# A Mamba block and a mixture of experts on one core: the steps of a chunk's projections, turns, norms and scatters laid out anew

## The chip, the cores and the metric

One core of one Trainium2 chip. The metric is the device time of one execution in microseconds, the median of the runs shown. The core has TensorE (matmuls and transposes, results to PSUM), VectorE, ScalarE (called ACT here), GpSimd, and a queue that issues DMAs (SyncE). Each engine works off its own instructions strictly in the order in which they were given, and waits on semaphores that the others raise.

## The reference

Input x is 8 sequences of 1024 tokens with 256 features, f32. Two stages follow each other:

```
n   = layernorm(x)                         # without weights
h   = layernorm(n, ln_g, ln_b)
x_in, z = split(h @ W_in)                  # 256 -> 2 x 512
u   = silu(causal_conv(x_in, 4 taps) + conv_b)
dt, B, C = split(u @ W_xproj)              # 64 + 16 + 16
delta = softplus(dt @ W_dt + b_dt)
s_t = exp(delta_t * A) * s_(t-1) + delta_t * B_t * u_t     # 512 channels x 16 states
y_t = sum over states of s_t * C_t, + u * D_param
x1  = x + n + (y * silu(z)) @ W_out
r   = layernorm(x1)
out = x1 + layernorm(r + top-2-of-8 experts(r), gamma, beta)
```

Routing takes the two largest of eight logits of `r` and weighs two experts (256 to 512, relu, back to 256) with a softmax of the two.

## The kernel before

**Chunks, groups and steps.** `mamba_block` cuts the tokens into 16 chunks of 512 (`NC`). An even chunk begins a sequence, an odd one goes on with it, so its scans start from states that the even one saved (`carry`). A chunk has four groups of 128 channels (`G`), a group has 16 states (`N`). One state of one group over 512 tokens is one scan instruction on VectorE, so a chunk has 64 steps (`SG`), numbered here 0 to 63. Step 19, say, is state 3 of group 1. GpSimd has half steps (two states at once, `HB` = 8 for a group, 32 for a chunk). Each engine runs its own written-out loop over the steps (`for at in range(STEPS)`); the step at which an instruction is given fixes only its place in that engine's order. Time comes from the waits.

**What a step needs.** For scan n, ACT makes the decay `exp(delta * A)` (`exp_a`, L1053). GpSimd makes the product with B for two states (`times_b`, L764), but not for states 4, 5, 10 and 11: their products come from TensorE ("drives", L1343, of `duT` and the diagonals `dg`). VectorE scans (L612). The states are weighed with C: ten of 16 by VectorE in five instructions (`weigh`, L624), six by GpSimd in three (L781; called W0, W1 and W2 here, given at the half steps of `WEIGH_P`; W2 needs scan 15 of its group and is given in the next group's half steps). TensorE turns each weighed pair into `ps_y` by eight transposes ("turn 0" to "turn 4" of VectorE's pairs, `TURN_D`, and of GpSimd's, `TURN_P`). `begin_y` (`SKIP_Y`) starts `ps_y` with the skip term, called y0 here. When all eight turns of a group are in, VectorE's `gate` (L634, state 3 of the next group) multiplies `ps_y` with silu(z). The product delta * u of the next group (`times_u`, L751, called U) is on GpSimd, given at half step `DU_AT`; it is transposed by TensorE ("turnu").

**The two slots of ps_p.** Everything else on TensorE goes through two PSUM banks in turn (`proj`, by place in `table`; `emptied` tells which semaphore says that a bank was taken): "h" (transposes of the normalised tile), "x" and "z" (the two halves of W_in), "conv", "dbc", "bturn", "dt", "turnu", "back" (transposes of the gated output), "out" (W_out and the residual), and for the previous chunk's routing "turnx", "logit" and "rank". A project of the table can start when the one two places ahead is emptied. A row of `STEADY` is (kind, group, chunk relative to this one, step, in how many parts, lag): TensorE is given part p at step + p, and ACT (VectorE for the last pass of dt) empties it at step + lag, ahead of the decay of that step. So where ACT empties a bank, its decays for later scans stand behind it. At one step TensorE is given the turns and drives first and then the projects.

**Other steps.** ACT: the silu of z for a whole chunk (`SILU_Z`, two table loads round it), the silu of u (`SILU_U`), the residual's base at step 12 (`residual_base`, L939), the norm of a chunk two ahead (`NORM`, waits for GpSimd's `factors`), the routed norm (`STATS_X1`, `INV_STD_X1`, `XN`), the diagonals (`DIAGONALS`, L1006), the routing weights (`EXP_W`) and the columns with weight and row number (`IDS_0`, `IDS_1`). In even chunks ACT also copies the end state of each pair that it will go over (`keep`, L1060, at step 2 and 9 of a group for the pairs whose bank a drive takes, `KEEP_EARLY`), and the drive waits for that copy. VectorE: last pass of softplus (`ADD_DT`), norm statistics (`STATS`) and 14 small routing instructions (`ROUTE`, the last one, L567, casts the row numbers). GpSimd: `factors` (`FACTOR`), `factors_x1` (`FACTOR_X1`) and eight scatters of 128 routed rows (`SCATTER`, half step, which of the two experts, tile; L738).

After the last chunk `moe_block` runs the experts over the sorted rows and writes the output.

## Time and profile before

| | |
|---|---|
| median of 3 runs | 2513.48 us (2511.04 to 2518.06) |
| the profiled execution | 2514.33 us |
| its span, first to last instruction | 2512.3 us |
| steady chunk, even / odd (6 / 7) | 114.8 / 114.0 us |
| scans of chunk 0 start / last scan ends | 45.9 / 1872.1 us |
| mean granted clock of TensorE | 0.949 |

Times of the trace are microseconds from the first instruction. The row of a group of like instructions gives the start of the first, its length, engine, line, what it writes and reads, and in brackets the idle time of the engine just before it and what ended that. Lengths of neighbouring matmul groups overlap by about 0.15 us; the difference of starts is what they take. At full clock TensorE runs at 2.4 GHz, at half (0.5) at 1.2.

### The profile page before, as it was taken

The numbers are of one execution on the slowest core, as the hardware profiler recorded it, in microseconds if no ns is written. First come the engines' busy times: TensorE is split into PE (matmuls) and PEld (weight loads), VectorE is DVE, ScalarE is ACT, GpSimd is POOL, SyncE is SP. The second block draws the span as 40 slices with busy tenths as digits, with TensorE's granted clock in tenths as the row PEclk, the third lists the DMA queues.
The fourth block names the chain that finished last, engine by engine and source line by source line (L and its number), as shares of the span: only waits on it lengthen the run. The fifth ranks groups of instructions, "written<-read, shape, count | busy, mean of one in ns | idle before, by whom it ended". The sixth has DMA issues, their size and how long they took to land. (4 is left out here: it accounts for less than half of the span.)

```text
span 2512.3 us, 46699 instructions
## 1 busy us (share of the span) xinstructions
PE 2271.6 (90%) x13655; PEld 1796.7 (72%) x13656; DVE 2060.2 (82%) x3040; ACT 1554.0 (62%) x3488; POOL 1746.7 (70%) x1105
## 2 busy tenths in 40 slices
PE   5989898998989898988989898989775999999988
PEld 2667666766767676767767776767674999999973
DVE  4999898989998999989889989989973555556557
ACT  5687777878786877778787767777642221222217
POOL 2787978888898879888888979798961222222227
PEclk8999999999999999999999999999886999999999
DMA  4031413314040313223140414132226777777769
GB/s 166 1 136 40 131 53 109 100 62 138 24 152 32 132 41 129 72 90 122 40 153 9 152 36 135 48 113 84 70 87 186 225 224 229 229 230 230 225 195 338
DMA packets 173511, 311.97 MB, mean 124 GB/s; under 512 B 19043, under 2 KB 100483, under 8 KB 173220
## 3 DMA queue, kind: packets, MB, share of 16 engines
q1 hardware_dynamic: 140132, 256.68, 33.0%
q0 software_dynamic: 12624, 34.62, 3.6%
q10 hardware_dynamic: 20592, 18.65, 2.2%
q8 instruction: 84, 1.38, 0.2%
q14 instruction: 79, 0.65, 0.1%
HBM read 255.47 MB, written 54.41 MB: 123 GB/s over the span
## 5 line engine op out<-in xcount | busy, mean ns | idle before, releaser
L764 POOL TENSOR_TENSOR dbu<-du,bb 128x1024 f32<-128x1024 f32 x384 | 901.5, 2361 | 88.3 <-DVE ps_a L612 83.1
L1053 ACT ACTIVATE ps_a<-dl,a_neg 128x512 f32<-128x512 f32 x768 | 515.3, 687 | 106.2 <-DVE ss L612 94.9
L781 POOL TENSOR_TENSOR wp<-ss,rows_c 128x1024 f32<-128x1024 f32 x192 | 453.4, 2361 | 69.8 <-DVE ss L612 69.8
L1621 POOL DMA_INDIRECT eo_scratch<-ow,idx x135 | 129.4, 959 | 391.2 <-DVE ow L1575 385.3
L624 DVE TENSOR_TENSOR wd<-ps_a,rows_c 128x1024 f32<-128x1024 f32 x320 | 382.8, 1196 | 0.0
L1316 PE MATMUL ps_y<-ident,wd 128*128 128x128 f32 x2560 | 344.9, 279 | 24.6 <-DVE wd L624 24.4
L1316 PEld LDWEIGHTS ps_y<-ident,wd 128*128 128x128 f32 x2560 | 302.7, 145 | 82.0 <-issue 49.3
L1343 PEld LDWEIGHTS ps_a<-dg,duT 128*128 128x128 f32 x2048 | 262.0, 203 | 58.9 <-issue 57.6
L1343 PE MATMUL ps_a<-dg,duT 128*128 128x128 f32 x2048 | 271.0, 288 | 10.1 <-DVE wd L624 5.8
L1660 ACT COPY e_meta<-xt 128x2 f32<-128x2 f32 x135 | 26.0, 192 | 400.9 <-PE e_ps_x L1721 400.9
L1326 PE MATMUL ps_y<-ident,wp 128*128 128x128 f32 x1536 | 213.7, 285 | 61.7 <-POOL wp L781 61.7
L1730 PE MATMUL e_ps_h<-xT,w 128*128 128x128 f32 x2160 | 264.8, 276 | 0.0
L1561 DVE TENSOR_SCALAR e_hT<-e_ps_h,b_turned 128x128 f32<-128x128 f32 x540 | 152.0, 344 | 135.1 <-PE e_ps_h L1730 135.1
L1739 PE MATMUL e_ps_o<-rows_c,e_hT 128*128 x1080 | 255.3, 379 | 0.0
L1730 PEld LDWEIGHTS e_ps_h<-xT,w 128*128 128x128 f32 x2160 | 253.5, 193 | 0.1
L1326 PEld LDWEIGHTS ps_y<-ident,wp 128*128 128x128 f32 x1536 | 184.1, 147 | 93.1 <-POOL wp L781 69.2
L612 DVE TENSOR_TENSOR_SCAN ss<-ps_a,carry,dbu 128x512 f32<-128x512 f32 x192 | 242.2, 1261 | 6.1 <-POOL dbu L764 5.0
L612 DVE TENSOR_TENSOR_SCAN ps_a<-ps_a,carry,dbu 128x512 f32<-128x512 f32 x192 | 236.8, 1270 | 2.8 <-ACT ps_a L1053 2.0
L612 DVE TENSOR_TENSOR_SCAN ss<-ps_a,dbu 128x512 f32<-128x512 f32 x192 | 230.3, 1200 | 4.7 <-ACT ps_a L1053 4.6
L612 DVE TENSOR_TENSOR_SCAN ps_a<-ps_a,dbu 128x512 f32<-128x512 f32 x192 | 225.3, 1211 | 6.4 <-ACT ps_a L1053 6.4
L1220 PE MATMUL ps_p<-xin,taps 128*128 128x512 f32 x480 | 225.7, 597 | 0.0
L1739 PEld LDWEIGHTS e_ps_o<-rows_c,e_hT 128*128 128x128 f32 x1080 | 195.1, 191 | 20.8
(196 smaller groups left out, 3823.6 us busy)
## 6 DMA issues: line engine op xcount, KB each, us to landing
w<-in_L_ffn_W_dram SPq DMA_DIRECT2D x135, 512.0 KB, 4.2
rows_c<-b_scratch SPq DMA_DIRECT2D x128, 512.0 KB, 5.6
bb<-b_scratch SPq DMA_DIRECT2D x96, 512.0 KB, 3.9
xt<-xs_scratch SPq DMA_DIRECT2D x135, 129.0 KB, 3.3
ee<-eo_scratch SPq DMA_DIRECT2D x64, 256.0 KB, 6.7
xb<-in_L_attn_x_dram SPq DMA_DIRECT2D x16, 512.0 KB, 4.0
hx<-in_L_attn_x_dram SPq DMA_DIRECT2D x16, 512.0 KB, 6.8
x_scratch<-hx SPq DMA_DIRECT2D x16, 512.0 KB, 2.9
```

What stands on the lines that cost most here:

```text
L612: dve.tensor_tensor_scan(dst, decay, drive, init, ALU.mult, ALU.add).then_inc(scan_done, 1)
L624: dve.tensor_tensor(wd[:, s % NWD], states(k, 2), cc[:, n:n + 2, :], ALU.mult).then_inc(wd_done, 1)
L764: pool.tensor_tensor(dbu[:, k % NBU], du[:, g % 2, :].unsqueeze(1).broadcast_to([P, 2, CH]), bb[:, row:row + 2, :], ALU.mult).then_inc(dbu ...
L781: pool.tensor_tensor(wp[:, s % 2], ss[:, s % 2], cc[:, rows, :], ALU.mult).then_inc(wp_done, 1)
L1053: act.activation(dst, dl[:, g, :], ACT.Exp, scale=a_neg[:, g, n:n + 1]).then_inc(exp_done, 1)
L1220: ins = pe.matmul(dst, taps[:, g, k, :], xin[:, g, k:k + CH], start=(k == 0), stop=(k == TAPS - 1))
L1316: ins = pe.matmul(ps_y[:, i, :], wd[:, s % NWD, h, i * P:(i + 1) * P], ident[:], start=False, stop=False, is_transpose=True, skip_group_ch ...
L1326: ins = pe.matmul(ps_y[:, i, :], wp[:, s % 2, h, i * P:(i + 1) * P], ident[:], start=False, stop=(j == 2 and h == 1 and i == NT - 1), is_t ...
L1343: ins = pe.matmul(ps_a[:, bank(k), i * P:(i + 1) * P], duT[:, i, :], dg[:, p, h, i, :], start=True, stop=True)
L1561: ins = dve.tensor_scalar(hT[:, 1 - par, j, :], ps_h[:, 1 - par, j, :], b1t[:, bass.ds(e * KF + j, 1)], 0.0, ALU.add, ALU.max)
L1730: ins = pe.matmul(ps_h[:, 1 - par, j, :], w1[:, (slot + 3) % RING, k, j * P:(j + 1) * P], xT[:, 1 - par, k, :], start=(k == 0), stop=(k == ...
L1739: ins = pe.matmul(ps_o[:, par, 0:D], hT[:, par, k, :], w2[:, bass.ds((e * KF + k) * D, D)], start=(k == 0), stop=(k == KF - 1))
```

## The change

The same instructions with the same operands are given at other steps. In `STEADY` almost every row moves. What moves farthest: x0 from steps 4 and 5 to 7 and 8, back3 stays at 6 and is now ahead of x0; out0 from one part at 10 to two at 11 and 12; out1 from 14 to 17; x1 from 17 to 14; x2 from 24 and 25 to 20 in one part; conv0 from 18 and 19 to 22 in one part, with lag 0 in place of 2; h0 and h1 both at 0; turnu3, dt0, dt1 one later; z1 to z3 two or three later, each with its turnu0 and back2. The silu of z goes from step 70 (step 6 of the chunk it is for) to 73 (step 9). NORM goes from 53 and 58 to 59 and 60 and GpSimd's FACTOR from half step 27 to 30. Scatters go from half steps 25, 26, 26, 27, 28, 29, 30, 33 to 25, 26, 26, 28, 30, 30, 33, 37. W0 to W2 go from half steps 4, 7, 9 to 5, 8, 10, so W1 comes behind the next group's first B product, and W2 behind a scatter given at half step 25 or 33. U goes from 5 to 7, behind both last B products. Turn 1 of GpSimd's goes from 19 to 16.

```diff
-        STEADY = [("h", 0, 1, 0, 1, 3), ("h", 1, 1, 1, 1, 5), ("x", 0, 1, 4, 2, 3), ("back", 3, -1, 6, 1, 2),
-                  ("dt", 2, 0, 9, 1, 2), ("out", 0, -1, 10, 1, 4), ("turnu", 1, 0, 10, 1, 5),
-                  ("out", 1, -1, 14, 2, 4), ("x", 1, 1, 17, 1, 5), ("conv", 0, 1, 18, 2, 2), ("conv", 1, 1, 21, 2, 5),
-                  ("x", 2, 1, 24, 2, 3), ("x", 3, 1, 25, 1, 4), ("dt", 3, 0, 29, 1, 2), ("conv", 2, 1, 27, 3, 5),
-                  ("turnu", 2, 0, 33, 1, 4), ("conv", 3, 1, 30, 4, 8), ("turnx", 0, -1, 37, 1, 4),
-                  ("turnx", 1, -1, 37, 1, 4), ("logit", 0, -1, 40, 1, 0), ("dbc", 0, 1, 41, 1, 4),
-                  ("back", 0, 0, 42, 1, 3), ("bturn", 0, 1, 43, 1, 3), ("rank", 0, -1, 43, 1, 1),
-                  ("back", 1, 0, 45, 1, 3), ("turnu", 3, 0, 47, 1, 1), ("dt", 0, 1, 48, 1, 1), ("dt", 1, 1, 49, 1, 2),
-                  ("z", 0, 1, 53, 2, 2), ("z", 1, 1, 54, 2, 4), ("z", 2, 1, 56, 2, 5), ("turnu", 0, 1, 59, 1, 2),
-                  ("z", 3, 1, 59, 2, 4), ("back", 2, 0, 60, 1, 4)]
+        STEADY = [("h", 0, 1, 0, 1, 5), ("h", 1, 1, 0, 1, 5), ("back", 3, -1, 6, 1, 3), ("x", 0, 1, 7, 2, 3),
+                  ("dt", 2, 0, 9, 1, 2), ("out", 0, -1, 11, 2, 3), ("turnu", 1, 0, 12, 1, 4), ("x", 1, 1, 14, 1, 6),
+                  ("out", 1, -1, 17, 2, 4), ("x", 2, 1, 20, 1, 1), ("conv", 0, 1, 22, 1, 0), ("conv", 1, 1, 22, 2, 4),
+                  ("x", 3, 1, 24, 1, 6), ("dt", 3, 0, 28, 1, 2), ("conv", 2, 1, 27, 3, 5), ("turnu", 2, 0, 33, 1, 5),
+                  ("conv", 3, 1, 30, 4, 8), ("turnx", 0, -1, 37, 1, 4), ("turnx", 1, -1, 37, 1, 4),
+                  ("logit", 0, -1, 40, 1, 2), ("dbc", 0, 1, 41, 1, 4), ("bturn", 0, 1, 42, 1, 3),
+                  ("back", 0, 0, 42, 1, 4), ("rank", 0, -1, 44, 1, 0), ("back", 1, 0, 44, 1, 4),
+                  ("turnu", 3, 0, 48, 1, 0), ("dt", 0, 1, 49, 1, 0), ("dt", 1, 1, 50, 1, 2), ("z", 0, 1, 53, 2, 1),
+                  ("z", 1, 1, 56, 1, 4), ("z", 2, 1, 59, 2, 3), ("turnu", 0, 1, 60, 1, 2), ("back", 2, 0, 61, 1, 3),
+                  ("z", 3, 1, 60, 2, 4)]
-        SILU_Z = 70
-        NORM = (53, 58)
-        ADD_DT = ((50, 0), (51, 1), (75, 2), (96, 3))
+        SILU_Z = 73
+        NORM = (59, 60)
+        ADD_DT = ((49, 0), (52, 1), (75, 2), (95, 3))
-        STATS = (47, 48)
-        INV_STD = (51, 53, 54)
-        FACTOR = 27
-        STATS_X1 = (27, 27)
-        INV_STD_X1 = (27, 28)
-        FACTOR_X1 = 15
-        XN = (35, 38)
+        STATS = (48, 48)
+        INV_STD = (51, 51, 53)
+        FACTOR = 30
+        STATS_X1 = (23, 25)
+        INV_STD_X1 = (31, 31)
+        FACTOR_X1 = 17
+        XN = (32, 38)
-        EXP_W = (42, 43, 43)
-        IDS_0 = 44
-        IDS_1 = 55
-        SCATTER = ((25, 0, 0), (26, 0, 1), (26, 0, 2), (27, 0, 3), (28, 1, 0), (29, 1, 1), (30, 1, 2), (33, 1, 3))
-        DIAGONALS = (53, 59, 64, 64)
+        EXP_W = (44, 44, 46)
+        IDS_0 = 47
+        IDS_1 = 56
+        SCATTER = ((25, 0, 0), (26, 0, 1), (26, 0, 2), (28, 0, 3), (30, 1, 0), (30, 1, 1), (33, 1, 2), (37, 1, 3))
+        DIAGONALS = (52, 55, 59, 62)
...
-        TURN_D = {9: 0, 10: 1, 14: 2, 17: 3, 20: 4}
-        TURN_P = {10: 0, 19: 1, 20: 2}
-        SKIP_Y = 7
-        WEIGH_P = {4: 0, 7: 1, 9: 2}
-        DU_AT = 5
+        TURN_D = {9: 0, 11: 1, 14: 2, 17: 3, 20: 4}
+        TURN_P = {10: 0, 16: 1, 20: 2}
+        SKIP_Y = 8
+        WEIGH_P = {5: 0, 8: 1, 10: 2}
+        DU_AT = 7
...
                 q = due(at, FACTOR, 2, G * HB)
-                if q is not None:
+                if q is not None and q > 1:
                     factors(q)
```

`ROUTE` moves some of its small instructions by a step or two, and `RESIDUAL` is not used.

## Rows read from the trace of the kernel before

**Rows 1.** The page: busy time and share of the engines, TensorE's granted clock.

```profile
PE 2271.6 (90%) x13655; PEld 1796.7 (72%) x13656; DVE 2060.2 (82%) x3040; ACT 1554.0 (62%) x3488; POOL 1746.7 (70%) x1105
...
PEclk8999999999999999999999999999886999999999
```

**Rows 2.** Windows: length; PE, PEld, DVE, ACT, POOL busy; granted clock, DMA share, GB/s.

```profile
737.60:781.10 43.50, 43.31 (x236) 33.42 (x237) 36.02 (x35) 29.23 (x62) 38.89 (x23) 0.95 0.14 52
781.10:818.70 37.60, 36.64 (x232) 27.69 (x231) 35.13 (x45) 28.52 (x59) 27.60 (x17) 0.95 0.13 45
818.70:852.70 34.00, 25.75 (x164) 18.88 (x162) 32.80 (x38) 31.29 (x76) 32.35 (x23) 0.97 0.54 183
852.70:896.50 43.80, 43.75 (x237) 33.58 (x238) 37.30 (x35) 27.79 (x55) 38.17 (x18) 0.94 0.16 52
```

**Rows 3.** VectorE's waits, 733.2 to 962.0: us in total, times, longest.

```profile
DVE ps_a L612 <- PE ps_a L1343: 7.1, 7, 1.4
DVE zt L634 <- PE ps_y L1316: 5.8, 2, 3.4
```

**Rows 4.** Timeline of GpSimd, 818.5 to 856.

```profile
818.80 0.18 POOL L775 COPY carry<-ss 128x2 f32<-128x2 f32 x1 [4.12 <-DVE ss L612]
...
821.46 1.02 POOL L738 DMA_INDIRECT xs_scratch<-stage,sli  x1
...
825.03 2.37 POOL L764 TENSOR_TENSOR dbu<-du,bb 128x1024 f32<-128x1024 f32 x1
...
850.36 2.33 POOL L781 TENSOR_TENSOR wp<-ss,rows_c 128x1024 f32<-128x1024 f32 x1
```

**Rows 5.** Windows as above, 841.7 to 857.7.

```profile
841.70:850.80 9.10, 5.37 (x45) 4.66 (x43) 8.52 (x9) 8.44 (x22) 9.10 (x7) 1.00 0.74 254
850.90:857.70 6.80, 4.95 (x18) 4.15 (x19) 4.96 (x5) 6.21 (x6) 6.61 (x4) 0.50 0.65 199
```

**Rows 6.** Timeline of TensorE, 733 to 783 and 836 to 905.

```profile
737.64 1.97 PE L1326 MATMUL ps_y<-ident,wp 128*128 128x128 f32 x8 [3.18 <-POOL wp L781]
...
847.49 1.09 PE L1316 MATMUL ps_y<-ident,wd 128*128 128x128 f32 x8 [0.68 <-DVE wd L624]
852.75 1.97 PE L1326 MATMUL ps_y<-ident,wp 128*128 128x128 f32 x8 [4.17 <-POOL wp L781]
854.51 1.92 PE L1343 MATMUL ps_a<-dg,duT 128*128 128x128 f32 x8
856.22 1.76 PE L1209 MATMUL ps_p<-turned_h,win 128*128 128x512 f32 x2
857.81 1.05 PE L1343 MATMUL ps_a<-dg,duT 128*128 128x128 f32 x8
...
886.72 3.60 PE L1220 MATMUL ps_p<-xin,taps 128*128 128x512 f32 x8
890.16 1.05 PE L1307 MATMUL ps_y<-skipd,xc 128*128 128x128 f32 x8
```

**Rows 7.** Timeline of ACT, 733 to 785 and 849 to 872.

```profile
746.81 0.16 ACT L1060 COPY carry<-ps_a 128x2 f32<-128x2 f32 x1
...
768.02 0.69 ACT L963 ACTIVATE xc<-ps_p,cb 128x512 f32<-128x512 f32 x1 [4.67 <-PE ps_p L1220]
...
851.96 1.28 ACT L1037 ACT_TABLE_LOAD   x1
...
856.47 0.69 ACT L1053 ACTIVATE ps_a<-dl,a_neg 128x512 f32<-128x512 f32 x1
...
864.28 2.07 ACT L939 ACTIVATE hx<-hx,nb,sc 128x256 f32<-128x256 f32 x4
```

**Rows 8.** Timeline of VectorE, 815 to 819 and 848 to 900.

```profile
817.44 0.17 DVE L567 CAST sli<-ps_p 128x8 uint32<-128x8 f32 x1
...
888.40 1.26 DVE L612 TENSOR_TENSOR_SCAN ss<-ps_a,carry,dbu 128x512 f32<-128x512 f32 x1
...
896.46 2.51 DVE L612 TENSOR_TENSOR_SCAN ps_a<-dbu,carry,ps_a 128x512 f32<-128x512 f32 x2 [1.03 <-PE ps_a L1343]
```

More of the change, by code:

```diff
@@ L267, in mamba_block @@
         SILU_U = 41
-        SILU_Z = 70
-        NORM = (53, 58)
-        ADD_DT = ((50, 0), (51, 1), (75, 2), (96, 3))
-        RESIDUAL = ((1, 0), (32, 1))
-        STATS = (47, 48)
-        INV_STD = (51, 53, 54)
-        FACTOR = 27
-        STATS_X1 = (27, 27)
-        INV_STD_X1 = (27, 28)
-        FACTOR_X1 = 15
-        XN = (35, 38)
-        ROUTE = (38, 38, 38, 39, 39, 39, 39, 39, 39, 42, 45, 46, 46, 46)
-        EXP_W = (42, 43, 43)
-        IDS_0 = 44
-        IDS_1 = 55
-        SCATTER = ((25, 0, 0), (26, 0, 1), (26, 0, 2), (27, 0, 3), (28, 1, 0), (29, 1, 1), (30, 1, 2), (33, 1, 3))
-        DIAGONALS = (53, 59, 64, 64)
+        SILU_Z = 73
+        NORM = (59, 60)
+        ADD_DT = ((49, 0), (52, 1), (75, 2), (95, 3))
+        RESIDUAL = ((4, 0), (24, 1))
+        STATS = (48, 48)
[5 more added lines that the diff above has]
+        XN = (32, 38)
+        ROUTE = (38, 39, 39, 40, 40, 40, 40, 40, 40, 41, 45, 46, 46, 46)
+        EXP_W = (44, 44, 46)
[3 more added lines that the diff above has]
+        DIAGONALS = (52, 55, 59, 62)
         DRIVE = (4, 5, 10, 10)
```

## The prediction

> **What bounds the kernel now.** The page comes first: TensorE, VectorE and GpSimd are all busy 70 to 90% of the span and TensorE's granted clock is nearly always full [rows 1], so no single engine is the bound and the answer must come from one chunk. I then asked the trace for two neighbouring chunks of the middle (chunk 6, in which a sequence begins, and chunk 7, in which the scans take their start from the stored states; 733.2 to 962.0 us). They last 114.8 and 114.0 us and repeat to 0.3 us up to chunk 13. Each falls into three legs. Read the busy columns in [rows 2] and see which engine fills each leg:
>
> - leg A, from the end of scan 47 to the end of GpSimd's last weighing of the chunk ("W2", which by then lies at step 2 of the next chunk): 34.0 us. GpSimd works 32.35 us of it, and after W2 of the group before (818.8) the trace shows it waiting for nothing but its own issues [rows 4]. TensorE has 8 us idle in it. At its end TensorE waits 4.17 us for W2 [rows 6].
> - leg B, from W2 to scan 26: 43.8 us (43.5 in chunk 6), TensorE busy for 43.75. VectorE's waits for TensorE lie here: in two chunks 5.8 us for the turns ahead of the gate of step 19 and most of the 7.1 us for the drives [rows 3].
> - leg C, scan 26 to scan 47: VectorE, 35.13 us busy of 37.6 in chunk 6.
>
> A microsecond is gained only in the engine that fills the leg. VectorE's waits in leg B are not worth their sum: TensorE is behind, and takes a wait away in one place only to bring it in another.
>
> TensorE's clock fell to half for 6.8 us at W2 [rows 5]. The price: W2's eight transposes 1.97 us against 1.09 for the eight just before, the drive 1.92 against 1.05, the half of x0 1.59 from its start to the next against 0.86 (a quarter of conv1's 3.44): 0.88 + 0.87 + 0.73 = 2.5 us per chunk, on TensorE's own leg [rows 6]. In chunk 6, where the fall began earlier in the wait, it is 2.0.
>
> **Leg A, after.** GpSimd's chain has seven scatters in it now. Three together take 821.46 to 825.03, 1.19 each [rows 4]. In the new order one scatter (half step 25) stands ahead of the W2 of step 50, where GpSimd idles 4.12 us for scan 47; the one at 27 goes to 28, 28 and 29 to 30, 30 to 33 and the last to 37, behind the leg's end. So six remain. The first needs the row numbers, which VectorE casts by 817.61 [rows 8]; its 1.02 us end at 818.8, where W2's work now begins, at most 0.1 late. Net -1.1 us. Bounds: -1.2, and 0 if the row weights (now copied at ACT step 47, not 44) come late. The du product moved behind two B products (5 to 7), and W1 behind the next B0, are the same work in another order; U has TensorE's turnu0 (step 60) queued behind it, with z3, back2, h0, h1 and five turns after that, and these must be done before W2. By the durations above they are, by 2 us. NORM and FACTOR (53, 27 to 59, 30) and the diagonals take away a short wait of scan 53 and crowd ACT at steps 59 to 62. Both lie under GpSimd's chain: 0, and up to 0.5 if that cover is gone.
>
> **Leg B, after.** The same TensorE work stands ahead of the drive of step 26 in both orders, so moving x0 behind the second drive, turn 1 from 19 to 16, out1 behind x1 and conv0 from 18 to 22 takes waits off VectorE at steps 5 and 19 [rows 3] but not one instruction off TensorE. What counts are new waits.
>
> (1) conv0 now has lag 0: ACT empties it at step 22 before the decay of scan 22. Today TensorE reaches conv1 at 886.72 and scan 22 starts at 888.40. In the new order x2 (half of a conv, 1.72) is ahead too and conv0 is last: 888.44, its end 0.15 later, the evacuation 0.69, the decay 0.69 [rows 6, 7]: 889.9, or +1.5. From scan 22 to 26 there are 8.06 us now, 1.03 of them waiting for the drives [rows 8]; those are ready then, and the squares for the norm (now at ACT step 25, 2.8 us of ACT) delay scan 25 by 0.3. So 7.4, -0.7. Sum +0.8 (chunk 6: +0.9).
>
> For the next three I go along TensorE's order with 0.9 us for eight transposes or a drive (1.05 less the 0.15 that the next overlaps), 0.4 for four, 1.7 for x or half a conv, and along ACT's with 0.7 for a decay and 0.6 for an evacuation, at full clock.
>
> (2) The silu of z goes from step 6 to step 9. It holds ACT for 4.5 us, two table loads included (851.96 to 856.47) [rows 7]. Today that lies under VectorE's waits at steps 3 to 5. Behind it now come the residual (2.07 us, step 12) and the softplus of dt2. TensorE's out0 waits for the residual. From W2 at 851.6 TensorE does the turn, two drives (854.4), back3, x0, y0, turn 0, dt2, two drives, two turns and four matmuls of out0 and would be at that point at about 864.9. ACT evacuates back3 (855.8), does the silu (860.3), three decays, x0, dt2's first pass and the residual: 865.6. +0.7.
> (3) back3 now stands right behind the drives, ahead of x0, and waits for the gate, which VectorE ends at about 854.1: between 0 and 0.4. I take 0.4, since scans 0 to 3 are not sped up for certain.
> (4) In even chunks the two states that step 9 saves (copied at 746.81 today [rows 7]) come out behind the silu, and the drives of step 10 wait for the copy. By the same walk from W2 at 736.5 TensorE is there at 744.2 (turn, two drives, back3, x0, y0, turn 0, dt2), and ACT, with back3 evacuated at 741.2 and 4.5 us of silu, at 745.9: +1.7, with (2) and (3) then down to 0.4.
>
> So before the clock: odd chunks +0.8 + 1.1 = +1.9, even +0.9 + 2.1 = +3.0.
>
> **The clock.** At full clock through W2, 2.5 and 2.0 come back. Will it stay? TensorE's wait ahead of W2 was 3.18 and 4.17 us in the two chunks [rows 6]. In the new order turn 1, h0, h1 and turn 3 come later, after U, and W2 comes 1.1 earlier: I count 2.1 to 2.4 us of wait. That is shorter, but part of the idle time only moves to around turnu0, and I do not expect it to keep the clock every time. A fall of half today's length costs 3.4/2 = 1.7, of which waits (2) to (4) hide 0.4 (odd) or 0.9 (even).
>
> The row also bears on a rule of the Trainium skill ("TensorE: Matmul & The Clock Gate", Part 4, PE-mode transpose), that the full clock does not engage for transposes, which don't count as busy in the same way. The trace disagrees: from 841.7 to 850.8 TensorE ran little but transposes at a granted clock of 1.00 [rows 5], and eight took 1.09 there and 1.97 at half. By that rule of the Trainium skill the fall at W2 would stay as long as it is, since all that comes ahead of it are transposes, and the time would be the slow rival's below.
>
> **Leg C, after.** Dbc, turns and drives keep their order; bturn, back0 and rank trade places (rank up to 0.4 earlier), the first half of the routed norm goes from 35 to 32. Even: the routed tile's norm is 0.2 later on ACT and the rank earlier, about 0; odd: VectorE fills it. 0, bounds -0.4 and +0.5. The guard on factors changes no step of the loop (the chunk number is 2 or more there). EXP_W, ROUTE, IDS and INV_STD move tiny instructions within their slack.
>
> **Sum for a pair of chunks.** Leg A -1.1 twice. Clock full throughout: even -1.1 + 3.0 - 2.0 = -0.1, odd -1.1 + 1.9 - 2.5 = -1.7: -1.8. Half-length falls: +0.7 and -0.4: +0.3. I take the mean of the two, -0.7. Seven pairs (chunk 0 and the last have no such join or another table; the tail from 1872 us and the experts' part don't change): -5 us. The profiled execution took 2514.3 (span 2512.3), 0.8 over the median, so 2509.
>
> **Rivals.**
> - R1, the clock stays up everywhere: -1.8 x 7 = -13, 2502. For it: the wait ahead of W2 gets shorter by a third or more. Against: the idle time of leg A is not gone.
> - R2, ACT is far enough ahead, so that (1) to (4) cost nothing and TensorE's leg shrinks by its clock alone: -1.1 - 1.3 = -2.4 for each of 14 chunks, -34, 2480. Against it: lag 0 at step 22 and VectorE and ACT in step there today (ACT waits 4.67 us for this conv [rows 7]).
> - R3, slower: the clock falls at W2 for as long as today, so nothing of the 4.5 us per pair comes back, while the silu's and conv0's waits are new. They hide 1.4 of it: -1.8 + 4.5 - 1.4 = +1.3 per pair, +9, 2523. It decides where the wait ahead of W2 stays above some 3 us. That rule of the Trainium skill would have it so.
> - R4, the first scatter is late (its weights or numbers), and W2 is not earlier: +1.1 x 14 = +15, 2524.
>
> **Chances.** Forecast 0.40, R1 0.26, R2 0.10, R3 0.16, R4 0.08. A tenth or so of the forecast's own spread falls below 2506. Within 0.3% is about what this kernel's measurement can tell from no change (2506 to 2521). Faster 0.42, same 0.38, slower 0.20. The range 2488 to 2524 leaves out R2's far end and little above R4. The likeliest case alone: 2503 to 2516.
>
> **What would show it.** In the changed profile: VectorE's wait at the gate of step 19 gone, and in its place one of about 3 us ahead of scan 22, put down to ACT; the wait for W2 at 2 to 2.5 us; leg A at 33 us; ACT's residual ending at 17 to 18 us into the chunk. I am wrong if scan 22 doesn't wait (R2), if leg A is not shorter (R4), or if waits of over 1 us stand at scans 9 to 11 or 60 to 63, which would say that ACT, and not TensorE, sets leg B or has outgrown its cover in leg A.

## The result, and the profile after

The changed kernel takes 2490.96 us (median; 2490.2 to 2494.66) beside 2515.27 us of the kernel before on the same chip (2511.04 to 2518.06). The ratio is 0.9907, 95% interval 0.9893 to 0.9922: faster by 0.9%. That lies inside the range of the prediction (2488 to 2524) and on the side it thought likeliest, but 18 us below its likeliest value of 2509, and below the own range of that case (2503 to 2516). So the steps have to be looked at one by one. The profiled execution has a span of 2492.6 us against 2512.3.

The page of the changed kernel, busy time by engine and TensorE's granted clock in 40 slices (for [rows 1]):

```profile
PE 2256.4 (91%) x13655; PEld 1779.9 (71%) x13656; DVE 2060.0 (83%) x3040; ACT 1561.9 (63%) x3488; POOL 1750.7 (70%) x1105
...
PEclk8999999999999999999999999999986999999999
```

VectorE and GpSimd do the same work in the same time. TensorE is busy for 15.2 us less with the same 13,655 matmuls: the first sign that part of the gain is clock and not order. The page's digits can't show it, the legs can. Chunks 6 and 7 run from 727.9 to 953.0 us now and last 112.8 and 112.3 us (before 114.8 and 114.0). The same legs as in [rows 2], windows with their length, busy times of PE, PEld, DVE, ACT and POOL, granted clock, DMA share and GB/s; B of chunk 6, C of 6, A into 7, B of 7, C of 7:

```profile
731.20:776.30 45.10, 43.67 (x242) 33.92 (x243) 37.17 (x36) 32.21 (x66) 36.30 (x22) 0.96 0.18 55
776.30:811.30 35.00, 34.90 (x237) 27.48 (x236) 34.57 (x46) 27.23 (x55) 31.23 (x20) 1.00 0.13 42
811.30:844.40 33.10, 24.65 (x154) 18.01 (x151) 32.08 (x38) 29.85 (x74) 31.64 (x24) 1.00 0.54 190
844.40:887.10 42.70, 42.15 (x241) 32.10 (x242) 38.01 (x35) 31.00 (x59) 35.86 (x17) 1.00 0.19 57
887.10:923.90 36.80, 36.79 (x238) 28.16 (x238) 36.02 (x46) 26.62 (x48) 30.70 (x16) 0.95 0.15 46
```

Put beside [rows 2]: leg A 33.1 for 34.0; leg B of the odd chunk 42.7 for 43.8; leg B of the even chunk 45.1 for 43.5, longer; leg C of the even chunk 35.0 for 37.6; leg C of the odd chunk 36.8 for 36.4. The largest single difference, -2.6 us, is in the leg for which the prediction had nothing. In that window the granted clock is 1.00 where it was 0.95.

VectorE's waits in the two chunks, in total, times and longest (for [rows 3]):

```profile
DVE ss L612 <- ACT ps_a L1053: 7.8, 4, 3.5
DVE dl L584 <- ACT dl L1024: 2.1, 2, 1.3
DVE ps_a L612 <- PE ps_a L1343: 2.1, 3, 0.8
DVE ps_a L612 <- ACT dbu L1053: 1.8, 1, 1.8
```

The gate's 5.8 us are gone and the drives' 7.1 are down to 2.1. In their place VectorE waits for ScalarE: 3.1 and 3.5 us ahead of scan 22 for its decay, as the timeline of VectorE shows (for [rows 8]), 1.8 us ahead of scan 21 of chunk 6, and 0.9 and 1.3 us at step 11, for ScalarE's pass of dt2.

```profile
875.73 1.29 DVE L612 TENSOR_TENSOR_SCAN ps_a<-dbu,carry,ps_a 128x512 f32<-128x512 f32 x1 [0.73 <-PE ps_a L1343]
880.12 1.28 DVE L612 TENSOR_TENSOR_SCAN ss<-ps_a,carry,dbu 128x512 f32<-128x512 f32 x1 [3.11 <-ACT ps_a L1053]
```

TensorE at the two starts of a chunk (for [rows 6]) and through dbc of chunk 6:

```profile
731.28 1.97 PE L1326 MATMUL ps_y<-ident,wp 128*128 128x128 f32 x8 [2.02 <-POOL wp L781]
...
741.91 2.02 PE L1343 MATMUL ps_a<-dg,duT 128*128 128x128 f32 x16 [1.35 <-ACT carry L1060]
...
797.82 3.64 PE L1226 MATMUL ps_p<-xc,wxp 128*96 128x512 f32 x8
...
844.42 1.09 PE L1326 MATMUL ps_y<-ident,wp 128*128 128x128 f32 x8 [2.12 <-POOL wp L781]
...
847.34 0.63 PE L1271 MATMUL ps_p<-ident,zt 128*128 128x128 f32 x4
```

W2's turning takes 1.09 us in chunk 7 where it took 1.97, and still 1.97 in chunk 6. The windows of the clock say the same (for [rows 5]), with TensorE's clock at 1.00, 2.4 GHz, right through the start of chunk 7 and at 0.50, 1.2 GHz, for 3.4 us in chunk 6:

```profile
731.30:734.70 3.40, 3.40 (x16) 3.40 (x17) 2.85 (x4) 2.82 (x6) 3.40 (x2) 0.50 0.83 189
...
841.00:848.00 7.00, 4.84 (x41) 4.44 (x40) 7.00 (x7) 6.26 (x11) 6.99 (x5) 1.00 0.81 240
```

The kernel before had a second fall in its even chunks that I had not looked at, and here are its rows, windows and TensorE's timeline of the kernel before:

```profile
803.10:806.50 3.40, 3.29 (x6) 1.24 (x5) 3.30 (x9) 3.34 (x9) 2.20 (x1) 0.50 0.00 0
```

```profile
803.38 5.19 PE L1226 MATMUL ps_p<-xc,wxp 128*96 128x512 f32 x8
```

The eight matmuls of dbc took 5.19 us there and 3.64 us after the change (797.82 above). Behind them stand the drives of step 42, for which VectorE waited 0.91 us (VectorE's timeline of the kernel before), and the rank, for which it waited 0.64 at step 45:

```profile
809.49 1.23 DVE L612 TENSOR_TENSOR_SCAN ps_a<-dbu,ps_a 128x512 f32<-128x512 f32 x1 [0.91 <-PE ps_a L1343]
```

But this fall did not leave dbc, it changed chunks. In chunk 7 dbc ran at full clock before the change and runs at half clock for 3.4 us (from 908.8) after it, and so it is in the odd chunks 3 to 13. TensorE's timelines of chunk 7, before and after:

```profile
918.57 3.65 PE L1226 MATMUL ps_p<-xc,wxp 128*96 128x512 f32 x8
```

```profile
908.67 5.34 PE L1226 MATMUL ps_p<-xc,wxp 128*96 128x512 f32 x8
```

Leg C of chunk 7 is only 0.4 us longer all the same.

GpSimd's timeline at both ends of leg A (for [rows 4]):

```profile
810.48 1.02 POOL L738 DMA_INDIRECT xs_scratch<-stage,sli  x1 [1.37 <-DVE sli L567]
811.51 0.20 POOL L775 COPY carry<-ss 128x2 f32<-128x2 f32 x1
...
821.33 1.01 POOL L738 DMA_INDIRECT xs_scratch<-stage,sli  x1 [0.17 <-issue]
...
822.50 2.36 POOL L781 TENSOR_TENSOR wp<-ss,rows_c 128x1024 f32<-128x1024 f32 x1
...
842.02 2.35 POOL L781 TENSOR_TENSOR wp<-ss,rows_c 128x1024 f32<-128x1024 f32 x1
```

One scatter stands in GpSimd's idle time now, right behind the row numbers, and W2 of the chunk ends at 844.37, 33.04 after scan 47 (33.96 before). ScalarE's rows of chunk 6 that steps (2) and (4) spoke of (for [rows 7]):

```profile
736.86 1.28 ACT L1037 ACT_TABLE_LOAD   x1
...
741.39 0.16 ACT L1060 COPY carry<-ps_a 128x2 f32<-128x2 f32 x1
...
744.26 2.08 ACT L939 ACTIVATE hx<-hx,nb,sc 128x256 f32<-128x256 f32 x4
```

The silu is at 736.86, the state copy comes out behind it at 741.39, and the drives of step 10 start at 741.91 after waiting 1.35 for it.

### The profile page after: what moved, and what is told of

It reads as the page before. It is cut to its first block and busy times, and to the rows that moved or that the text cites. A ratio compares the mean times of both kernels' runs of the same rounds, so it can differ in the third digit from the quotient of the medians.

```text
span 2492.6 us, 46699 instructions
## 1 busy us (share of the span) xinstructions
PE 2256.4 (91%) x13655; PEld 1779.9 (71%) x13656; DVE 2060.0 (83%) x3040; ACT 1561.9 (63%) x3488; POOL 1750.7 (70%) x1105
## 5 line engine op out<-in xcount | busy, mean ns | idle before, releaser
L1316 PE MATMUL ps_y<-ident,wd 128*128 128x128 f32 x2560 | 338.1, 277 | 3.5 <-DVE wd L624 3.5
L1343 PEld LDWEIGHTS ps_a<-dg,duT 128*128 128x128 f32 x2048 | 253.3, 199 | 61.6 <-issue 59.4
L1343 PE MATMUL ps_a<-dg,duT 128*128 128x128 f32 x2048 | 264.5, 283 | 32.5 <-ACT carry L1060 25.1
L612 DVE TENSOR_TENSOR_SCAN ss<-ps_a,dbu 128x512 f32<-128x512 f32 x192 | 231.8, 1207 | 36.7 <-ACT ps_a L1053 35.5
```

What stands on the lines that cost most here:

```text
L612: dve.tensor_tensor_scan(dst, decay, drive, init, ALU.mult, ALU.add).then_inc(scan_done, 1)
L1316: ins = pe.matmul(ps_y[:, i, :], wd[:, s % NWD, h, i * P:(i + 1) * P], ident[:], start=False, stop=False, is_transpose=True, skip_group_ch ...
L1343: ins = pe.matmul(ps_a[:, bank(k), i * P:(i + 1) * P], duT[:, i, :], dg[:, p, h, i, :], start=True, stop=True)
```

## The experiments

Their times are medians, each beside the kernel before in the same session (2513.3 to 2514.0 us); that of the changed kernel is from its own session, beside 2515.3. Legs are the means over the even (e) and odd (o) chunks 4 to 13, each leg A counted with the chunk that it leads into, its length from the end of scan 47 to the end of W2, and so on as in the prediction. To 0.1 us:

```
                 median   A e   A o   B e   B o   C e   C o
before            -       33.5  34.0  43.4  43.8  37.7  36.4
changed          2491.0   32.7  33.4  44.4  43.0  35.6  36.8
lag 2            2487.5   32.7  33.4  43.0  42.4  36.7  36.9
silu z at 6      2489.4   33.0  33.6  43.3  43.6  36.1  36.3
both             2488.6   32.6  33.5  43.0  43.0  36.7  36.6
bturn only       2511.2   33.5  34.0  43.6  44.0  37.3  36.4
h three times    2513.1   33.5  34.0  43.4  43.9  37.8  36.4
new list only    2526.5   33.6  34.3  45.0  44.1  36.8  36.2
old list back    2558.5   32.9  33.3  49.0  45.0  37.4  38.0
scatters only    2575.9   36.3  37.0  46.7  45.4  36.4  36.4
 + meta at 57    2551.2   36.5  36.8  45.6  43.6  36.1  36.4
scatters back    2603.1   36.0  36.6  45.1  44.6  39.7  39.0
before + filler  2518.1   33.5  34.0  45.6  43.2  36.4  36.7
lag 2 + filler   2530.2   32.6  33.3  46.4  45.1  36.8  37.1
```

**Is VectorE's wait ahead of scan 22 worth its length?** The changed kernel with conv0's lag back at 2:

```diff
-("conv", 0, 1, 22, 1, 0)
+("conv", 0, 1, 22, 1, 2)
```

> The changed kernel with one number back: ACT empties conv0 at step 24 (lag 2), behind the decays of scans 22 and 23, not ahead of them. Legs theory: the wait of 3.1 us at scan 22 goes, but TensorE's work ahead of the drive of step 26 is the same; in odd chunks TensorE has the drive of step 26 ready about 1 us before scan 26 begins, so at most 1 us per chunk is gained and the rest comes back as a wait at scan 26: -5 to -15 us against the changed kernel (ratio to before 0.985 to 0.989). VectorE's waits theory: 3.1 us in each of 14 chunks, -43 us (ratio 0.974).

Measured 2487.53 us, ratio 0.9895 (0.9879 to 0.9912). The wait of 3.1 to 3.5 us at scan 22 is gone from all chunks, and the kernel gains some 3 us, neither the 43 of the waits theory nor the 5 to 15 of the legs theory. VectorE's waits in a stretch of three chunks of this run:

```profile
DVE ps_a L612 <- PE ps_a L1343: 7.4, 7, 1.5
DVE ss L612 <- ACT ps_a L1053: 4.7, 6, 1.2
```

The drives' wait is back, 1.5 us at scan 26, and a wait for ScalarE of 1.0 to 1.2 stands at scan 25. Leg B is 0.6 shorter in the odd chunks and, without the fall at W2 there, 1.5 in the even ones; but leg C of the even chunks gives 1.1 back, since the clock falls at dbc instead. TensorE fills leg B, and a wait of VectorE's is worth little there: the prediction's reading holds. The price it gave to lag 0, 0.8 to 0.9 us, does not: set beside the changed kernel's even chunks without a fall at W2 (4 and 14, 43.2 and 43.3), lag 2 has 43.0, so lag 0 costs some 0.3 there and 0.4 to 0.6 in the odd chunks. The interval overlaps that of the changed kernel, so the 3 us are not shown.

**Does the later silu cost?** The changed kernel with silu z at the step it had (step 6 of the chunk).

```diff
-        SILU_Z = 73
+        SILU_Z = 70
```

> The changed kernel with the silu of z back at step 6. My prediction's price of that move: 1.7 to 2.1 us in even chunks (the drives of step 10 wait for the copy of the states behind the silu) and 0.7 in odd ones (out0 waits for the residual), so with TensorE setting leg B -2.4 to -2.8 per pair, -17 to -20 us against the changed kernel (ratio to before 0.983). Rival: at step 6 the silu stands ahead of back3's evacuation and of the decays 6 to 8, VectorE waits 1 to 2 us at scans 6 to 8 in its place, and nothing is gained (0.991).

Measured 2489.38 us, ratio 0.9908 (0.9891 to 0.9924): nothing, as the rival said. The waits ahead of scan 9 (0.4 to 0.5 us in even chunks) and at step 11 go, and in their place scan 6 waits 1.1 to 1.3, as VectorE's waits in three chunks show:

```profile
DVE ss L612 <- issue: 3.8, 3, 1.3
```

The clock has to be set apart here: this run has no fall at W2 in chunks 2 to 14, and its leg B of the even chunks is 43.1 to 43.5, while the changed kernel's is 43.2 and 43.3 in the two that have no fall there either (4 and 14). ScalarE's 4.5 us of silu have to stand somewhere; in the even chunks of this order the place does not matter. In the odd ones step 6 is 0.6 worse in leg B (43.6 against 43.0) and 0.5 better in leg C, where two of the five chunks (7 and 9) have no fall at dbc: 35.9 there, 36.6 in the others. Both edits together:

> Both together. Legs theory: the gains add up until VectorE sets leg B (its busy time there is 36 to 37 us of 43 to 44): -22 to -35 us against the changed kernel, ratio to before 0.977 to 0.982. If one hides the other: as the better of the two alone.

Measured 2488.56 us, ratio 0.9911 (0.9894 to 0.9927): the two don't add up. It also shows what a fall at dbc costs in the new order: the odd chunks with one (7 and 9) have 37.1 in leg C, those without (3, 5, 11 and 13) 36.2.

**Leg C: is it bturn ahead of back0?** The kernel before with that alone:

```diff
-("back", 0, 0, 42, 1, 3), ("bturn", 0, 1, 43, 1, 3)
+("bturn", 0, 1, 42, 1, 3), ("back", 0, 0, 42, 1, 4)
```

> The kernel before with bturn put ahead of back0 at step 42, nothing else: the only part of the change that I expected to act in leg C. If the shorter leg C of even chunks (37.6 to 35.4 us) comes from this order: the wait of 0.6 us for the rank at step 45 goes and even chunks gain 0.4 to 0.6, -4 us. If it comes from the clock, which stands full through dbc in the changed kernel: leg C stays 37.6 and the time within 2 us of before.

Measured 2511.22 us, ratio 0.9992 (0.9982 to 1.0002). Leg C of the even chunks goes from 37.65 to 37.25, since the pick of step 45 waits 0.22 for the rank instead of 0.64. The fall of the clock at dbc stays. So this order is worth 0.4 us in each even chunk's leg C, the bound that the prediction had named, too little to stand clear of the noise in the time, and it is not what took 2 us.

**The scatters and GpSimd's order alone.** The kernel before with the new half steps of the scatters and of W2:

```diff
-        SCATTER = ((25, 0, 0), (26, 0, 1), (26, 0, 2), (27, 0, 3), (28, 1, 0), (29, 1, 1), (30, 1, 2), (33, 1, 3))
+        SCATTER = ((25, 0, 0), (26, 0, 1), (26, 0, 2), (28, 0, 3), (30, 1, 0), (30, 1, 1), (33, 1, 2), (37, 1, 3))
-        WEIGH_P = {4: 0, 7: 1, 9: 2}
+        WEIGH_P = {4: 0, 7: 1, 10: 2}
```

> The kernel before, and of the change only the steps of the scatters and W2 one half step later. Legs theory (GpSimd sets leg A, TensorE leg B, each order keeps the work): leg A 1.0 to 1.1 us shorter in each of 14 chunks, -15 us; TensorE's wait ahead of W2 falls from 3.2 and 4.2 to 2.1 and 3.1, and where that keeps the clock full another 2 us per chunk comes back, up to -30 more. Rival, VectorE's waits theory (only a wait taken off VectorE is worth something, and those of the gate and the drives are TensorE's order): within 3 us of before, since nothing moved on TensorE.

Measured 2575.87 us, ratio 1.0247 (1.023 to 1.0264): 62 us slower. Neither of the two had this. ScalarE, GpSimd and VectorE of this run, timelines:

```profile
978.40 0.85 ACT L916 ACTIVATE stage<-ex,wt 128x1 f32<-128x1 f32 x4 [7.86 <-DMA xs_scratch<-stage,sli]
```

```profile
971.24 1.01 POOL L738 DMA_INDIRECT xs_scratch<-stage,sli  x1 [0.16 <-issue]
...
980.12 1.01 POOL L738 DMA_INDIRECT xs_scratch<-stage,sli  x1 [4.25 <-ACT stage L917]
```

```profile
979.96 2.47 DVE L612 TENSOR_TENSOR_SCAN ps_a<-ps_a,carry,dbu 128x512 f32<-128x512 f32 x2 [6.05 <-ACT ps_a L1053]
```

The half step is not all of a scatter's place. At half step 28 the loop weighs W0 before it scatters, while in the changed kernel W0 has moved to half step 5 and stands behind (821.33 and 822.50 above). So the last scatter of the first half is issued later and lands 7.1 us after its issue. ScalarE at step 55 waits for that landing before it overwrites the weights' column in `stage`, and the decays are queued behind it: VectorE stands for 6.05 us. GpSimd in its turn waits 4.25 us for `stage`. With ScalarE's part moved from step 55 to 57:

```diff
-        IDS_1 = 55
+        IDS_1 = 57
```

> The kernel before with the new half steps of the scatters and of W2, as in the run that was 62 us slower, and ScalarE's making of the second half's columns moved from step 55 to 57. Theory 1 (that run lost its time because at step 55 ScalarE waits for the landing of the first half's last scatter, which the new half step 28 gives to GpSimd only after scan 55, and behind ScalarE in order stand the factors that VectorE scans with): ScalarE's wait of 7.4 us at steps 54 and 55 falls below 3 us, VectorE's wait of 6 to 7 us at step 55 is gone, time 2505 to 2525. Theory 2 (GpSimd's own order is the loss, whoever waits at step 55): 2550 and more.

Measured 2551.19 us, ratio 1.0147 (1.0132 to 1.0162). That is where the second theory had it (2550 and more). VectorE's wait fell from mostly 6 or 7 us to mostly 3.5 to 4.5, ScalarE's from some 7.5 only to some 6; the rest of the loss stays, because GpSimd's next scatter still waits for ScalarE (timeline of this run):

```profile
969.89 1.01 POOL L738 DMA_INDIRECT xs_scratch<-stage,sli  x1 [3.27 <-ACT stage L917]
```

The first theory named the right place and priced the cure wrongly, the second was right in the time and left ScalarE out: the two engines wait for each other in turn, and a later step of one only moves the wait. The opposite edit, in the changed kernel:

```diff
-        SCATTER = ((25, 0, 0), (26, 0, 1), (26, 0, 2), (28, 0, 3), (30, 1, 0), (30, 1, 1), (33, 1, 2), (37, 1, 3))
+        SCATTER = ((25, 0, 0), (26, 0, 1), (26, 0, 2), (27, 0, 3), (28, 1, 0), (29, 1, 1), (30, 1, 2), (33, 1, 3))
-        WEIGH_P = {5: 0, 8: 1, 10: 2}
+        WEIGH_P = {5: 0, 8: 1, 9: 2}
```

> The changed kernel with the scatters and W2 at their old half steps. Legs theory: leg A back to 33.5 and 34.0, +1.1 per chunk, +15 us against the changed kernel, TensorE's wait ahead of W2 longer by as much and the clock falling more often, up to +15 more: ratio to before 0.997 to 1.003. VectorE's waits theory: as the changed kernel, 0.991.

Measured 2603.07 us, ratio 1.0356 (1.0339 to 1.0374), slower than either kernel. GpSimd waits for `stage` at half step 28, which ScalarE fills at step 56 now, and the factors of half step 30, for which ScalarE has the norms at step 59 queued, are behind. Timelines of this run, GpSimd and ScalarE:

```profile
985.76 1.01 POOL L738 DMA_INDIRECT xs_scratch<-stage,sli  x1 [2.46 <-ACT stage L917]
...
992.68 0.20 POOL L726 TENSOR_TENSOR nb<-rr,nm 128x8 f32<-128x8 f32 x1
```

```profile
992.92 1.09 ACT L888 ACTIVATE hx<-xb,nb,rr 128x256 f32<-128x256 f32 x2 [6.09 <-POOL nb L726]
```

Leg A can thus not be had alone from either side. That its -0.9 does not hang on TensorE's list follows from the run with the old list, below.

**TensorE's list alone, and all but the list.** First the kernel before with the changed kernel's STEADY, TURN_D, TURN_P and SKIP_Y:

```diff
-        TURN_P = {10: 0, 19: 1, 20: 2}
+        TURN_P = {10: 0, 16: 1, 20: 2}
-        SKIP_Y = 7
+        SKIP_Y = 8
...
```

> The kernel before with TensorE's order and ACT's evacuations of the change (STEADY, TURN_D, TURN_P, SKIP_Y), all else as before (silu of z at step 6, scatters, U, norm). Legs theory: leg A as before, leg B +0.8 for conv0's lag 0 (a wait of 2.5 to 3 us at scan 22 replaces that of step 19), no wait of out0 or of the drives of step 10, and what the clock gives: +11 us at today's clock, -15 if it stays full. VectorE's waits theory: waits of 1 us at step 5 and 2.3 to 3.4 at step 19 go, so -30 us or more.

Measured 2526.54 us, ratio 1.0049 (1.0032 to 1.0066): slower by 13 us. It has the new waits of leg B (+1.6 in the even chunks, +0.3 in the odd ones) and not leg A's gain. VectorE also waits 2.9 to 3.3 us for dt1 in each chunk, since its own step for it (51) is still the old one and ScalarE's pass is at 52 now. And the clock is not what sets leg B of the even chunks here: it is 44.9 in chunks 4 and 10, with a fall of 3.4 us at W2, and in 8 and 12, without one. The legs theory had +11 with the long falls and -15 without any. Only short ones are left at W2 (in chunks 4, 6, 10, 11 and 14), and the run is 13 us slower: the theory is wrong for it. Then the changed kernel with the old list and turnings:

> The changed kernel with TensorE's list, its turnings and begin_y at the steps of before; GpSimd's, ScalarE's and VectorE's steps stay new. It is the counterpart of the run with the new list alone (13 us slower than before). Theory 1 (the gain is leg A's, GpSimd's, and the new list is worth little by itself): 2495 to 2505. Theory 2 (the old list keeps the long stretch at half clock at W2 and stands against the later norms and silu z; the gain is there only with both): 2512 and more, with the stretch at 0.50 back at steps 3 to 10. Theory 3 (the new list costs and the rest gains, as the two parts would add up from the run with the list alone): 2475 to 2482.

Measured 2558.54 us, ratio 1.0179 (1.0165 to 1.0194). Leg A is as short as in the changed kernel (32.9 and 33.3), so the part of the change that is not TensorE's list does that (GpSimd's steps, with ScalarE's and VectorE's); but leg B is 4.6 us longer than the changed kernel's in the even chunks and 2.0 in the odd ones. VectorE's waits in three chunks:

```profile
DVE zt L634 <- PE ps_y L1316: 9.4, 3, 3.7
DVE ss L612 <- ACT ps_a L1053: 7.0, 8, 2.1
```

The gate's wait is back in full, and waits for ScalarE's decays stand beside it. The second theory was right in sign and place (the gain is there only with both), but of the fall of the clock that it named only traces are there: in the even chunks it comes at 14 to 18 or 21 us, not at 3 to 10, and the odd chunks 3 to 13 have none there.

**What keeps the clock up at W2?** First the kernel before with the transposes of h given three times over, ahead of TensorE's wait:

```diff
+                    for again in range(3):
                         for i in range(NT):
                             ins = pe.transpose(dst[:, i * P:(i + 1) * P], hx[:, i, g * P:(g + 1) * P], ident[:])
```

> The kernel before with the eight transposes of h0 and h1 given three times over, 1.7 us more of TensorE per chunk, written into the same bank with the same result, all ahead of the wait for W2. Clock theory: TensorE has 8 us idle in leg A, so the work is free; if it keeps the granted clock full at W2, leg B gets 2.0 (even) and 2.5 us (odd) shorter, up to -30 us in all. Rival, the clock has no part in it (orders alone): the clock may or may not stay, and the time is within 3 us of before or some 5 us over it.

Measured 2513.13 us, ratio 0.9999 (0.999 to 1.0009). TensorE still waits 4.2 us for W2 in the odd chunks, and the clock still falls there for as long. In most even chunks it falls for 3.4 us instead of 6.8, and leg B is hardly shorter for it (43.2 for 43.5): the 3.4 us that are left are those with the drives in them. A window of this run, chunk 7:

```profile
851.30:858.10 6.80, 5.29 (x19) 4.26 (x20) 4.68 (x5) 5.88 (x6) 6.60 (x4) 0.50 0.62 210
```

It does not tell a rule for transposes from one for the wait's length. Next the wait itself is filled, with six matmuls of 128x512 that nobody reads, all else as before:

```diff
                     if n + N in TURN_P:
+                        if TURN_P[n + N] == 2 and t % G == 0 and 0 < t // G < NC - 1:
+                            u = place["x", 0, t // G + 1]
+                            pe.wait_ge(proj_free[u % 2], u // 2)
+                            for _ in range(6):
+                                pe.matmul(proj("x", 0, t // G + 1), win[:, 0, 0:P], win[:, 0, 0:CH],
+                                          start=True, stop=True)
                         turn_p(t - 1, TURN_P[n + N])
```

> The kernel before, with six matmuls of 128x512 (a block of the projection weights by another, into the bank that x 0 is about to overwrite, never read) put ahead of the turning of W2 at step 4 of each chunk, where TensorE waits 4.2 us (odd chunks) and 3.2 us (even chunks) for GpSimd today. At full clock six of them take some 3 us, so they fit into the wait; nothing else is changed. It asks what the fall of the granted clock at W2 costs by itself. Theory 1 (the fall follows TensorE's long wait, and it is worth what the prediction priced, 2.5 us in an odd chunk and 2.0 us in an even one): no stretch at 0.50 near steps 3 to 10, leg B (W2 to the start of scan 26) shorter by 2 us and more, chunks of some 112 us, time 2480 to 2490. Theory 2 (the fall has another cause, or what it delays is behind other limits): the stretch at 0.50 stays, or goes without leg B getting shorter by more than 0.5 us; time 2508 to 2516.

Measured 2518.09 us, ratio 1.0016 (1.0007 to 1.0025), slower by 4 us. The filler was mis-sized: six take 5.42 us, not 3, and overrun the wait. Timeline of TensorE, chunk 7 of this run:

```profile
849.20 5.42 PE L1357 MATMUL ps_p<-win 128*128 128x512 f32 x12 [0.82 <-ACT turned_h L947]
854.46 1.04 PE L1326 MATMUL ps_y<-ident,wp 128*128 128x128 f32 x8
```

It still gives the price. W2's turning starts at 854.46, 1.9 us after the end of W2 where it was 0.06 before, and is done with 1.04 instead of 1.97; leg B is 43.2 and thus 0.6 shorter all the same. If the delay goes whole to the end, the clock at W2 is worth 0.6 + 1.8 = 2.4 us in an odd chunk (the prediction had 2.5). In the even chunks the filler runs into a fall of 3.4 us itself, W2's turning is late by 4.0 us in the mean and leg B longer by 2.1: some 1.9 us, where the prediction had 2.0. The same run shows the price of the other fall in one program: chunk 5 had none at dbc, chunk 7 had one. The legs C of both, and the stretch of the fall at dbc of chunk 7:

```profile
666.90:703.30 36.40, 36.08 (x231) 28.61 (x230) 36.07 (x45) 27.48 (x51) 27.39 (x14) 0.95 0.14 45
895.70:933.50 37.80, 36.94 (x232) 27.71 (x232) 36.28 (x45) 28.04 (x52) 27.46 (x14) 0.95 0.14 45
...
917.90:921.30 3.40, 3.40 (x5) 1.30 (x6) 3.30 (x9) 3.32 (x7) 2.34 (x1) 0.54 0.01 2
```

```profile
689.01 3.65 PE L1226 MATMUL ps_p<-xc,wxp 128*96 128x512 f32 x8
...
917.85 5.34 PE L1226 MATMUL ps_p<-xc,wxp 128*96 128x512 f32 x8
```

Dbc 5.34 against 3.65, leg C 37.8 against 36.4: 1.4 us of leg for 1.7 of TensorE. Of the even chunks 4 to 12 chunk 8 alone has the fall, with 37.7 against 36.0 to 36.1: 1.6. Both legs above have a mean clock of 0.95, because leg C of chunk 5 has its fall too, later (from 699.8 us, where it costs nothing: the odd chunks of the run with bturn alone have no fall in leg C and last 36.4 as well). The mean clock of a window does not tell what a fall costs; what TensorE had to do in it does. Last, a smaller filler in the kernel with lag 2 (three matmuls, the rest of the edit as above). The expectation took a fall at the start of the even chunks to be left in that kernel, but the trace of lag 2 has none there in chunks 2 to 14:

> The changed kernel with lag 2 for conv 0 and three such matmuls of 128x512 ahead of W2, where TensorE waits 2.1 us in the even chunks and 1.3 us in the odd ones. Theory 1 (the stretch of 3.4 us at 0.50 that is left at the start of the even chunks goes, and with it some 1 us of each): 2480 to 2484, no stretch at 0.50 before step 10. Theory 2 (what W2's stretch delays is hidden now, or the filler itself is late and holds up W2's turning): 2486 to 2492.

Measured 2530.21 us, ratio 1.0058 (1.0046 to 1.007), outside both. Three matmuls take 2.8 us at full clock. In the even chunks they first wait 2.4 to 2.6 us for ScalarE, and in chunks 2, 8, 12 and 14 they then run at half clock, in a fall that was not there without them (4.38 us in chunk 8). Timeline of TensorE of this run:

```profile
977.25 4.38 PE L1357 MATMUL ps_p<-win 128*128 128x512 f32 x6 [2.40 <-ACT turned_h L947]
981.46 1.04 PE L1326 MATMUL ps_y<-ident,wp 128*128 128x128 f32 x8
```

W2's turning starts 3.2 us late in the mean of the odd chunks and 3.7 in the even ones, and leg B grows by 2.7 and 3.5 us. What delays W2's turning goes for the most part to the end (which takes the 2.4 of the filler's run down to 2.1 at the least). No version beat the changed kernel by more than the measurement tells.

## Why the prediction was right, and where it was not

**Leg A, -1.1: right.** Measured -0.9 into chunk 7 and -1.0 into chunks 6 and 8, by the mechanism named (one scatter in GpSimd's idle time, six left). In the mean of the odd chunks it is -0.6, for the late W2 of chunk 10. The run with the old list back has the same leg A. R4 is out.

**Leg B, (1) conv0's lag: the wait was right.** Predicted a wait of about 3 us ahead of scan 22; 3.1 and 3.5 measured. In the odd chunks +1.5 + 1.1 - 2.5 = +0.1 was foretold from W2 to scan 22, and the trace has 35.7 on both sides. From scan 22 to 26 I took -0.7; it is -1.1 (7.0 against 8.1). The run with lag 2 puts lag 0 at 0.3 to 0.6 us, not 0.8 to 0.9.

**(2) to (4): the waits are there, and with (1) they cost less than was counted.** The residual ends 18.5 us into chunk 6 (17 to 18 foretold) and TensorE waits 0.5 us for it in the odd chunks (0.7 foretold). Back3 did not wait for the gate (0 to 0.4, I took the 0.4). The drives of step 10 in the even chunk wait 1.35 us for the state copy behind the silu (1.7). Before the clock the prediction had +3.0 for (1) to (4) in the even chunks and +1.9 in the odd ones. Chunk 4, at full clock, is 0.4 shorter in leg B than before; with the 1.9 that the clock gave back that leaves +1.5. Chunk 7, 1.0 shorter, leaves +1.1 to +1.4 with 2.1 to 2.4. The prediction had named waits of over 1 us at scans 9 to 11 as a sign that ScalarE sets leg B: the wait for dt2 at step 11 is 1.3 us in chunk 6. The run with the silu moved back took it away and gained nothing, so the sign misled.

**The clock at W2: half right.** TensorE's wait ahead of W2 is 2.0 to 2.1 us, as counted (2.1 to 2.4). The forecast was the mean of a full clock and of a fall of half the length in every chunk. The fall is there in the even chunks 6, 8, 10 and 12 (3.4 us), absent in 4 and 14, and absent in the odd chunks 3 to 13, where the rival R1 had it right. Leg B odd, foretold at -0.6 with the clock full, measures -0.8 in the mean and -1.0 in chunk 7. The prices of the long fall, 2.5 and 2.0, are 2.1 to 2.4 and some 1.9 by the filler's run. But the fall of half the length costs 1.3 to 1.9 us in the changed kernel's even chunks (44.6 to 45.0 in leg B against 43.2 and 43.3), where the prediction took 0.8, since it let the waits hide half of it. The Trainium skill's rule ("TensorE: Matmul & The Clock Gate", Part 4, PE-mode transpose), by which transposes do not bring the full clock, is again not what the trace shows: in the changed kernel TensorE comes into the start of chunk 7 through transposes of h, wd and wp, and the clock stays at 1.00 over a wait of 2.12 us. R3, which hung on it, is out.

**Leg C, 0 with bounds -0.4 and +0.5: wrong for the even chunks, and this is the step that missed.** It measures -2.0 in the mean (35.6 against 37.7). I had read the clock at W2 alone and treated leg C as VectorE's, with TensorE's clock of no concern, though TensorE is busy for 36.64 of its 37.60 us in [rows 2]. The kernel before falls a second time in each even chunk, in dbc, behind which the drives of step 42, the turnings and the rank stand. That fall is gone in chunks 6, 8, 10 and 12, and the filler's run prices it at 1.6 in an even chunk. What is left, by chunk 4, which still has it: legs B and C of chunk 4 in the changed kernel,

```profile
506.70:549.80 43.10, 41.65 (x239) 31.90 (x240) 36.63 (x34) 31.61 (x66) 36.22 (x21) 1.00 0.15 54
549.80:586.50 36.70, 36.70 (x240) 28.74 (x239) 35.01 (x46) 27.13 (x54) 31.30 (x20) 0.95 0.14 46
```

so -1.0 with the fall in place, of which 0.4 is bturn ahead of back0 (measured by itself) and 0.6 is not traced further (TensorE's list alone does not give it: chunk 6 of that run, with the fall, has 37.7). Chunk 4 also shows a trade: without the fall at W2 its leg B is 43.1 and its leg C 36.7, while chunk 6 with it has 45.1 and 35.0. Either way B and C make about 80, because an even chunk now has one fall that costs, where it had two. Leg C of the odd chunks is 0.4 longer, inside the bound, but by luck: a fall in dbc is new there, which the prediction did not have. The runs with the silu at step 6 price it at 0.6 to 0.8, so that without it the leg would be some 0.2 to 0.5 shorter than before. Per pair of chunks the falls that cost went from three (two long ones at W2, one in dbc) to two short ones.

**The sum.** For a pair the prediction had -0.7: leg A -2.2, leg B +1.5 (the mean of +0.4 at full clock and +2.5), leg C 0. Chunks 4 to 9, three pairs, last 3.6 us less per pair: by the same legs -1.8, -0.3 and -1.5. So leg A was 0.4 too hopeful, leg C misses by 1.5, and leg B by 1.8. With the falls as the trace has them (half-length in chunks 6 and 8, none in 4, 5, 7 and 9) the prediction's own terms give +0.9 for leg B: 0.5 of the miss is the choice of the mean, and 1.2 the waits, which were taken too long by more than that, since the half-length falls cost more than counted. Seven such pairs would be -25; the last scan ends 20.6 us earlier, because chunk 0, taken as unchanged, is 2.4 longer (the leg A that leads out of it is 2.3 us longer, with TensorE at half clock for 6.8 us in it, from 144.2 us, where the kernel before had no fall; what makes it so was not looked into) and chunk 10 is 1.1 longer, with a late W2 behind it (leg A into chunk 11 is 34.9). Chunk 15, also taken as unchanged, is 2.7 shorter. The time is inside the range because the range is wide: 2491 lies between R1 (2502) and R2 (2480), and neither is what happened.

**Still open:** why the clock's falls sit where they do. Those in dbc come without any idle time of TensorE: it is busy for 36.79 of the 36.80 us of leg C of chunk 7, and just ahead of the fall at 908.8 it ran transposes and the logits' matmuls of 128x8. Whether those have a part in it was not tried. The shorter wait at W2 goes with no fall in the odd chunks, but chunks 4 and 6 have nearly the same work and differ, and more transposes ahead of the wait changed nothing in the odd chunks. Whether the filler's matmuls or the absence of a wait kept the clock in its odd chunks was not tried apart. Whether chunk 0 could keep its old order was not tried.

## What to carry to other kernels

Before a leg is given to one engine, list every fall of TensorE's clock in it and read what TensorE was doing in each: the same 3.4 us at half clock cost 0.6 to 1.6 in dbc, by what waited behind it, and nothing some 10 us later. In an order in which three engines wait for each other, a step is a place in a queue and not a time: ask what each moved instruction now stands behind, since TensorE's list or the scatters' steps, put alone into the old kernel, made it 0.5 to 2.5% slower, and put back alone in the new one 2.7 to 4.5%. A wait that a profile shows on the engine that is not the bound is worth little, as the 3 us at scan 22 were.

## What the runs showed of the hardware

A scatter's time from issue to landing varied by a factor of three. In chunk 7 of the kernel before, the three issued in a row land in 2.7, 2.4 and 2.6 us, the next four, between products, in 3.7, 6.8, 7.1 and 5.6. In the run with the scatters alone five of one chunk's land in 2.6 to 3.0 us and the one that ScalarE waited for in 7.1. What makes it so was not tried. An f32 matmul of 128x512 from constant operands counts as two in the records and takes 0.9 us at full clock (5.42 for six), which the filler should have been sized by.
